# A graph attention and expert kernel: how the first two supertiles are fed, where the row sums are made, and who splits the expert weights

## The reference

```python
h = inlayer2 @ W.T + b
f1 = h @ w1 + b1
f2 = h @ w2 + b2
logits = f1[:, None] + f2[None, :]
bias_mat = NEG_BIG * (1.0 - (adj_mat > 0))
coefs = softmax(leaky_relu(logits, 0.01) + bias_mat, axis=-1)
x = x + coefs @ layernorm(x)
xf = layernorm(x)
probs = softmax(xf @ gate_w + gate_b)          # top 2 of 8 kept, as weights cw
out = x + sum_e cw[:, e] * (gelu(xf @ W1[e] + b1[e]) @ W2[e] + b2[e])
```

## Time and profile before

| | |
|---|---|
| median of 3 runs | 521.17 us (520.91 to 521.98) |
| the profiled execution: its time | 521.97 us |
| its span, first to last instruction | 520.4 us |
| busy: PE / DVE / ACT / POOL | 474.6 / 437.2 / 211.1 / 55.1 us |
| mean granted TensorE clock | 0.969 |
| DMA queues, share of 16 engines over the span | GpSimd's 34.9%, SyncE's 22.0% |

### The profile page before, as it was taken

One profiled execution on the slowest core, in us unless ns is written; L12 is line 12 of the kernel. 1 busy time (PEld: TensorE's weight loads), 2 busy tenths in 40 slices (PEclk: granted clock), 3 DMA queues, 4 the chain that ended last, 5 costly groups with the idle time before them and its releaser, 6 DMA issues.

```text
span 520.4 us, 5922 instructions
## 1 busy us (share of the span) xinstructions
PE 474.6 (91%) x1760; PEld 232.5 (45%) x1760; DVE 437.2 (84%) x720; ACT 211.1 (41%) x322; POOL 55.1 (11%) x74
## 2 busy tenths in 40 slices
PE   1997879758999999999999999789999999999996
PEld 1976434413444544444444434334434444444442
DVE  0159379999999999999999998397989898988985
ACT  0127400001011110200102114579898888888884
POOL 5000410990200101010000000000000000000000
PEclk9997979789999999999999999979999999999999
DMA  6999999970393975929500000833443575534410
GB/s 132 195 168 117 213 166 147 92 72 1 26 105 33 89 72 46 105 15 104 52 0 0 0 0 9 148 95 66 116 82 101 97 124 110 116 101 101 120 60 22
DMA packets 36432, 44.47 MB, mean 85 GB/s; under 512 B 2320, under 2 KB 24768, under 8 KB 36416
## 3 DMA queue, kind: packets, MB, share of 16 engines
q0 software_dynamic: 16896, 16.78, 34.9%
q1 hardware_dynamic: 18704, 27.46, 22.0%
q10 hardware_dynamic: 816, 0.03, 0.1%
HBM read 92.38 MB, written 2.23 MB: 182 GB/s over the span
## 4 chain that ended last, share of the span: by engine, by line
PE 65%; DVE 16%; issue 7%; DMA 5%; ACT 4%; another core or an unknown queue 1%; SPq 1%; DVEq 1%; ACTq 0%
PE bank L1007 29%; DVE c L804 7%; PE bank L1045 4%; PE bank L1047 4%; PE bank L1046 4%; PE bank L1034 4%; PE bank L1035 4%; PE bank L1036 4%; DMA share<-in_L_gnn_inlayer 2%; PE bank L953 2%; PE bank L945 2%; PE bank L928 2%; DMA share<-shares 2%; ACT mask L544 2%; DVE xs L691 2%
## 5 line engine op out<-in xcount | busy, mean ns | idle before, releaser
L1007 PE MATMUL bank<-c,Y 128*128 128x512 f32 x512 | 234.9, 610 | 18.8 <-DVE c L804 18.7
L804 DVE SCALAR_TENSOR_TENSOR c<-g_row,r_col,maskT 128x512 f32<-128x512 uint8 (+1 forms) x256 | 196.1, 806 | 14.7 <-PE bank L1007 10.7
L1007 PEld LDWEIGHTS bank<-c,Y 128*128 128x128 f32 x512 | 94.5, 193 | 140.9 <-issue 81.5
L847 DVE TENSOR_TENSOR mask<-mask,share 128x1024 f32<-128x1024 f32 x64 | 78.3, 1223 | 23.1 <-ACT mask L544 16.1
L544 ACT ACTIVATE mask<-bank,b1T 128x512 f32<-128x512 f32 x128 | 83.8, 688 | 24.0 <-PE bank L1036 22.4
L853 DVE TENSOR_TENSOR maskT<-mask,maskT 128x1024 f16<-128x1024 f32 x64 | 78.3, 1224 | 0.0
L551 ACT ACTIVATE maskT<-mask 128x1024 f16<-128x1024 f32 x64 | 67.4, 1053 | 4.1 <-DVE mask L847 4.0
L1045 PE MATMUL bank<-maskT,w2h 128*128 128x512 f16 x128 | 49.1, 383 | 6.6 <-DVE maskT L853 6.1
L1035 PE MATMUL bank<-share,w1h 128*128 (+1 forms) x128 | 49.0, 383 | 0.0
L1046 PE MATMUL bank<-maskT,w2h 128*128 128x512 f16 x128 | 49.0, 383 | 0.0
L1047 PE MATMUL bank<-maskT,w2l 128*128 128x512 f16 x128 | 49.0, 383 | 0.0
(11 more groups left out here) (143 smaller groups left out, 343.9 us busy)
## 6 DMA issues: line engine op xcount, KB each, us to landing
mask<-in_adj POOLq DMA_DIRECT2D x32, 512.0 KB, 17.7
share<-shares SPq DMA_DIRECT2D x16, 1024.0 KB, 8.2
share<-in_L_gnn_inlayer SPq DMA_DIRECT2D x8, 256.0 KB, 8.7
share<-in_x SPq DMA_DIRECT2D x8, 256.0 KB, 20.1
out<-c SPq DMA_DIRECT2D x8, 256.0 KB, 3.8
share<-in_L_ffn_W SPq DMA_DIRECT2D x1, 1024.0 KB, 22.0
x<-in_x SPq DMA_DIRECT2D x1, 256.0 KB, 10.1
W_sb<-in_L_gnn_W SPq DMA_DIRECT2D x1, 64.0 KB, 1.9
```

The lines of the kernel that those rows point to most:

```text
L804: dve.scalar_tensor_tensor(c[:, k % CR].rearrange("p (s i) -> p s i", i=32), g_row[:, bass.ds(s * ST, ST)].rearrange("p (s i) -> p s i", i ...
L847: dve.tensor_tensor(hw[:, e % 2], h[:, e % 2], wb[:, e].unsqueeze(1).to_broadcast([P, FC, ST]), ALU.mult).then_inc(hw_done, 1)
L1007: mm(bank[:, par, :], Y[:, k], c[:, k % CR], start=(k == 0), stop=(k == NK - 1)).then_inc(c_used, 1)
```

## The change

- SyncE loads inlayer2 in plain rows (partition p has rows 32p to 32p+31, 8 KB in one run of each half) with two DMAs instead of eight. ScalarE alone copies the turned blocks, and puts the columns in the mask's order on the way. TensorE makes the f columns only after all eight blocks, 32 in a row.
- The first mask is loaded in 16 pieces (four quarters of four DMAs), each quarter with a semaphore of its own; VectorE turns the quarters between steps of the start. The second mask's DMAs are issued once x has landed.
- One f1 row is made before supertile 0, the other seven behind its chunks 1, 3, ... 13. ScalarE makes their `g_row` parts after its 24 rows of Y, and then the normalized rows `xin` of x (32 instructions), over `in2_j`.
- The row sums are eight products of ones by four `xin` chunks each, behind chunks 24 to 31 of supertile 0. VectorE makes `all_h` and `all_l` itself behind chunk 2 of supertile 1 (`mean_rows`).
- x2 is one DMA. The weights are loaded after supertile 0. ScalarE makes their high parts in supertile 1, VectorE the low parts in supertile 2 behind chunks 0, 3, ... 21.
- Supertiles 1 and 2 are taken out of the loops; gate and b2 are still split on GpSimd.

```diff
@@ sync
-            for b in (0, half):
-                for q in range(Q):
-                    sp.dma_start(dst_k(in2_j, q)[:, b:b + half],
-                                 by_chunk(in2)[q].rearrange("a b e d -> a b (e d)")[:, b:b + half]).then_inc(in2_in[b // half], 16)
+            for n in range(2):
+                part = slice(n * half, (n + 1) * half)
+                sp.dma_start(in2_j[:, part], by_k(in2)[:, part]).then_inc(in2_in[n], 16)
...
             sp.wait_ge(f1row_ready, NB)
-            sp.dma_start(x2[:, 0:TS], x_rows[:, 0:TS]).then_inc(xn_in[0], 16)
-            sp.dma_start(x2[:, TS:NK], x_rows[:, TS:NK]).then_inc(xn_in[1], 16)
+            sp.dma_start(x2[:], x.rearrange("(n p) d -> p n d", p=P)).then_inc(xn_in, 16)
+            sp.wait_ge(c_used, NK)
             sp.wait_ge(y_rows, NK + 1)
             sp.wait_ge(S_ready, 1)
@@ gpsimd
-            load_adj(0, 0)
+            for p in range(NP):
+                for q in range(Q):
+                    pool.dma_start(mask[32 * q:32 * q + 32, p],
+                                   adj_v[0, q][:, PS_ * p:PS_ * p + PS_]).then_inc(adj0_in[p], 16)
+            for n in range(2):
+                pool.wait_ge(xj_in[n], 64)
             load_adj(1, 1)
...
-            pool.wait_ge(S_step, 1)
-            pool.tensor_scalar(all_rows[:], all_rows[:], ident[:, D - 1:D], None, ALU.mult).then_inc(S_step, 1)
-            pool.wait_ge(S_step, 2)
-            pool.tensor_copy(all_h[:], all_rows[:]).then_inc(S_step, 1)
-            pool.wait_ge(S_step, 3)
-            pool.tensor_tensor(all_l[:], all_rows[:], all_h[:], ALU.subtract).then_inc(all_ready, 1)
...
             load_adj(3, 1)
-            split(w1raw, w1h[:], w1l[:], arrived=(w_in, 32))
-            split(w2raw, w2h[:], w2l[:])
@@ scalar
-            for b in range(1, NB, 2):
+            in2T_t = in2T.rearrange("d (b e q a1 a0) -> d a0 e q b a1", a0=8, e=4, q=Q, b=NB)
+            for b in range(NB):
                 act.wait_ge(in2t_ready, b + 1)
...
+                    if p == 6 and isinstance(s, int) and s == 1:
+                        act.wait_ge(w_in, 32)
+                        for raw, hi in ((w1raw, w1h[:]), (w2raw, w2h[:])):
+                            act.activation(hi, raw, ACT.Copy, scale=W_SCALE).then_inc(whi_made, 1)
...
             supertile(0, 0, first=True)
-            with act.Fori(0, NS // 2 - 1) as i:
+            for b in range(1, NB):
+                g_part(b)
+            for k in range(NK):
+                act.activation(xin[:, k], x_j[:, k], ACT.Identity, bias=nmrs[:, k:k + 1],
+                               scale=rs1[:, k:k + 1]).then_inc(xin_made, 1)
@@ vector
-            for b in range(0, NB, 2):
-                dve.wait_ge(in2t_ready, b + 1)
-                dve.tensor_copy(in2T[:, ST * b:ST * b + ST], bank[:, TURN[b % 4], :]).then_inc(in2t_dve, 1)
...
+                    if isinstance(s, int) and s == 1 and k == 2:
+                        mean_rows()
...
+                    if isinstance(s, int) and s == 2 and k % 3 == 0 and k < 24:
...
+                        dve.wait_ge(whi_made, v + 1)
+                        ins = dve.scalar_tensor_tensor(lo, raw, W_SCALE, hi, ALU.mult, ALU.subtract)
...
+            def mean_rows():
+
+                dve.wait_ge(S_ready, 1)
+                dve.wait_ge(pool_const, 1)
+                link(dve.tensor_reduce(all_rows[:], bank[:, 3, :].rearrange("p (e d) -> p d e", d=D), AX_X, ALU.add))
+                link(dve.tensor_scalar(all_rows[:], all_rows[:], ident[:, D - 1:D], None, ALU.mult))
+                link(dve.tensor_copy(all_h[:, 0:D], all_rows[:]))
+                dve.tensor_tensor(all_l[:, 0:D], all_rows[:], all_h[:, 0:D], ALU.subtract).then_inc(all_ready, 1)
@@ tensor
-            for k in range(NK):
-                ins = mm(bank[:, 3, P:P + D], rs1[:, k:k + 1].to_broadcast([P, P]), x_j[:, k],
-                         start=(k == 0), stop=(k == NK - 1))
-            ins.then_inc(S_ready, 1)
+            def row_sum(n):
+                pe.wait_ge(xin_made, 4 * n + 4)
+                return mm(bank[:, 3, :], ones[:], xin[:, 4 * n:4 * n + 4].rearrange("p k d -> p (k d)"),
+                          start=(n == 0), stop=(n == NK // 4 - 1))
...
+                    if first and k >= NK - NK // 4:
...
+                        ins = row_sum(k - NK + NK // 4)
...
+                    if first and k % 2 == 1 and k // 2 + 1 < NB:
+                        f1_row(k // 2 + 1)
```

More of the change, by code:

```diff
@@ L170, in gnn_moe_kernel @@
         out_sb = c[:, 1, :].rearrange("p (t d) -> p t d", d=D)
+        xin = in2_j
         in2T = x2[:, :, :].rearrange("p k d -> p (k d)")
@@ L181, in gnn_moe_kernel @@
         xj_in = [sem(f"xj_in{i}") for i in range(2)]
-        xn_in = [sem(f"xn_in{i}") for i in range(2)]
+        xn_in = sem("xn_in")
         w_in = sem("w_in")
         adj_in = [sem(f"adj_in{i}") for i in range(2)]
+        adj0_in = [sem(f"adj0_in{i}") for i in range(4)]
         pool_const = sem("pool_const")
@@ L207, in gnn_moe_kernel @@
         S_ready = sem("S_ready")
+        xin_made = sem("xin_made")
         all_ready = sem("all_ready")
@@ L211, in gnn_moe_kernel @@
         wsplit = sem("wsplit")
+        gate_split = sem("gate_split")
+        whi_made = sem("whi_made")
         b1_ready = sem("b1_ready")
@@ L285, in _ @@
         def _(sp):
-            half = NB // 2
+            half = NK // 2
             sp.dma_start(W_sb[:], gnn_w).then_inc(small_in, 16)
@@ L391, in _, with split @@
             splits = [0]
-            def split(raw, hi, lo, arrived=None):
-                if arrived is not None:
-                    pool.wait_ge(*arrived)
+            def split(raw, hi, lo, done):
                 n, splits[0] = splits[0], splits[0] + 1
@@ L614, in turn @@
             def turn(n, p, par):
-                dve.wait_ge(adj_in[par], 64 * n)
+                if isinstance(n, int) and n == 0:
+                    dve.wait_ge(adj0_in[p], 64)
+                else:
+                    dve.wait_ge(adj_in[par], 64 * n)
                 dve.transpose(at32v[:, par, PS_ * p:PS_ * p + PS_, :].rearrange("p s w -> p (s w)"),
@@ L623, in stats @@
                 return ins
-            dve.wait_ge(xj_in[0], 64)
-            stats(0, B1)
+            for n in range(2):
+                dve.wait_ge(xj_in[n], 64)
+                last = stats(n * B1, (n + 1) * B1)
+                if n == 0:
+                    turn(0, 0, 0)
+            link(last)
+            for k in range(NK):
+                ins = dve.bn_aggr(mv1[:, k], st1[:, k])
+            ins.then_inc(mv1_ready, 1)
+            turn(0, 1, 0)
             dve.wait_ge(fcol_made, 1)
-            f12 = bank[:, 4, 2 * P:2 * P + 2 * NK].rearrange("p (k v) -> p v k", v=2)
+            f12 = bank[:, 4, 32:32 + 2 * NK].rearrange("p (k v) -> p v k", v=2)
             dve.tensor_copy(f1_col[:], f12[:, 0])
@@ L671, in _ @@
                 row_chunk(k)
-            for p in range(2, NP):
-                turn(1, p, 0)
+            turn(0, 3, 0)
             POST = 3
@@ L797, in supertile @@
                         dve.wait_ge(turned, (s + 1) * NP)
-                    if first and k == 0:
-                        dve.wait_ge(grow_ready, NB)
+                    if k == 0:
+                        dve.wait_ge(grow_ready, 1 if first else NB)
                     need(dve, c_used, s * NK + k - CR + 1)
@@ L834, in supertile @@
                         next(router, None)
+            def mean_rows():
[5 more added lines that the diff above has]
+                dve.tensor_tensor(all_l[:, 0:D], all_rows[:], all_h[:, 0:D], ALU.subtract).then_inc(all_ready, 1)
             supertile(0, 0, 1, first=True)
-            with dve.Fori(0, NS // 2 - 1) as i:
-                supertile(i * 2 + 1, 1, i + 2)
+            supertile(1, 1, 1)
+            supertile(2, 0, 2)
+            with dve.Fori(1, NS // 2 - 1) as i:
+                supertile(i * 2 + 1, 1, i + 1)
                 supertile(i * 2 + 2, 0, i + 2)
```

130 lines of the change are left out of this document (63 added, 67 removed).

## The result

| | before | changed |
|---|---|---|
| median (lowest to highest), 4 runs each | 521.29 us (520.91 to 521.98) | 513.25 us (512.68 to 513.80) |
| span of the profiled execution | 520.4 us | 511.5 us |
| mean granted clock | 0.969 | 0.965 |

The ratio is 0.9844, with a 95% interval of 0.9827 to 0.9861: 8.0 us faster.

The account below looks back on a forecast made before the run. TensorE, then VectorE, nearly fill ordinary supertiles; GpSimd's splits and the wait for mask 1 cost extra. The -8.9 at supertile 3 and +0.5 gave -8.4: 513.6 from 521.97, 512.8 from the median; said 513.0, range 508.5 to 518.

Parts of the forecast that it names:

- Mask 1: Supertile 0: with x2, weights and mask 2 packets held back, mask 1 lands at 58.7 us, chunk 8 comes 7.1 earlier.
- the 1.1 us: Loads ahead of mask 1: 112 packets of mask 2 no longer moved before it, 1.1 us.
- rival 2: First mask in pieces is slower: 12 added DMAs make mask 1 8 us later, time 521; chance 0.05.
- End of supertile 0: TensorE done at 93.7 us: 91.2, less 7.1 for mask 1, plus 9.6 for three f1 rows and eight row sums.
- Rival 1: The start decides, not mask 1: supertile 0 ends at 95.2 or 98 us, time 514.5 to 517; chance 0.16.
- The start: Before supertile 0: first chunk at 51.6 us, supertile 0's end at 95.2, nearly level with mask 1's 93.7.
- Row sums into supertile 1: mean_rows takes 1.6 us, the rest of supertile 1 28.3; supertile 2 begins at 123.6 instead of 136.99, -13.4 in sum.
- Splits: High parts 4.2 us, hidden in supertile 1; low parts add 5.4 in supertile 2; supertile 3 at 159.4, -8.9.
- rival 4: More gain than forecast: low parts fall half into TensorE's time and mean_rows is cheap, 510 us; chance 0.11.
- After that: From supertile 3 on: TensorE bounds again with a shorter queue, +0.5 us given back; experts untouched.

Follow-up runs that it names:

- e9: The kernel before, with one wait added so that x2 and the weights load only after the first quarter of mask 1 is turned: 513.12 us.
- e10: The kernel before, with x2 and the weights held behind mask 1's first turn and the weight splits moved to ScalarE and VectorE: 501.71 us.
- e1: The changed kernel with the weight splits back on GpSimd and ScalarE's high and VectorE's low parts taken out: 524.25 us.
- e6: The changed kernel with the first mask in four DMAs instead of 16, all quarters waiting for the whole mask: 520.73 us.
- e3: The changed kernel without GpSimd's wait for x before it issues mask 1: 510.11 us.
- e2: The changed kernel with f1 rows reading in2T in runs of 32 adjacent columns and ScalarE ordering them as it writes g_row: 506.93 us.
- e5: The changed kernel with inlayer2 in eight DMAs of 2 KB a partition instead of two of 8 KB: 517.22 us.
- e4: The changed kernel with f1 rows read in runs of 32 columns and no wait for x before mask 1 is issued: 509.13 us.

## Why the prediction was right

It said 513.0 us, range 508.5 to 518; measured 513.25. The two causes hold by experiment (e9 and e10 for mask 1, e1 and e10 for the splits). That the number met the measured one within 0.3 us is luck: at supertile 3 the gain was 1.9 us short of the forecast, because the end of supertile 0 came later than said, and an unforecast gain of 1.9 us in the experts made up for it (in the profiled pair).

- **Mask 1, -7.1 predicted.** Chunk 8 came 8.1 us earlier, and mask 1 was in at 58.56 for the 58.7 of the sum. The cause is shown by e9, 6.4 us from the bytes in front of it; the sizes of the parts were off and cancelled. Mask 2 was issued at 50.06 us, earlier than before (60.86), so its packets were not out of the way: 133 of them had been moved by 58.5 us (4549 packets, less 2 x 2112 and the 192 that the pieces add), and the 1.1 us did not come. The faster start made up for it: by 56 us GpSimd's queue had moved 4.07 MB here and 3.92 in e9, beside the same 4.26 MB of SyncE's. The twelve more DMAs that rival 2 charged with 8 us cost nothing that shows (e6: 4.18 MB by 57 us with and without them).
- **End of supertile 0, "93.7 us"** (95.79 measured). This is the step that was wrong in kind: it let the mask decide, and took every wide product at 0.87 us. Four terms: chunk 8 ready 1.0 us sooner than I said; no gap, so none of the 1.6 to 1.9 us of slow clock (e9, e10) that stood unseen in the 91.2 us from the earlier trace rows; three f1 rows at 1.73 instead of 0.87, +2.6; TensorE, late from the start and from four earlier f1 rows, at chunk 8 only at 62.88 instead of 60.6, +2.3. That makes 2.0 to 2.3 for 2.1 measured. Rival 1's mechanism was therefore the true one, with a start earlier than its 51.6 us (first chunk at 46.3) and longer rows; the 512 columns alone did not fix an f1 row's price.
- **The start**, priced for a first chunk at 51.6 us, had it at 46.31: x came 7.4 us sooner, and GpSimd's late reduction (2.97 us of VectorE's time, e3) was not foreseen. Even so TensorE, and not the mask, decided.
- **Row sums into supertile 1.** `mean_rows` took 1.5 us (predicted 1.6), and the rest of the supertile 28.5 (28.3). No chunk there took over 0.75 us.
- **Splits.** High parts 1.9 us each (2.1), hidden. Supertile 2 was to take 35.8 us (30.4 of VectorE's work and waits, and 5.4 of low parts) and took 35.4. A low part has a record of 0.69 us, but the next instruction begins 0.60 us after it, so the eight are 4.8:

```profile
126.51 0.69 DVE L849 SCALAR_TENSOR_TENSOR w1l<-share,w1h 128x512 f16<-128x512 f32 x1
127.11 2.07 DVE L822 SCALAR_TENSOR_TENSOR c<-g_row,r_col,maskT 128x512 f32<-128x512 f32 x3
```

  Over an ordinary supertile of 31.3 they cost 4.1, since part of them falls into VectorE's slack, as rival 4 had it; the 30.4 of the sum had already counted 0.9 of that slack.
- **After that.** Supertile 3 began 7.0 us ahead of before instead of 8.9, and stayed so: 7.07 us at supertile 4. The "+0.5 given back" did not come.
- **A gain that was not forecast.** At VectorE's last chunk of supertile 7 the profiled pair is 7.0 us apart (325.35 and 318.32), at its first product of the experts 7.8 (334.39 and 326.57), and the spans 8.9. The difference comes in the experts' start, where before's profiled run also had a clock 0.08 lower for 21 us (0.84 and 0.92). That execution lay 0.7 us over its median, so part of it is that one run; the rest was not tried.

The prediction asked what the whole change gives, and not what each part gives alone. The two removed losses are worth some 20 us (e10), and some 11 to 12 of them are paid back by work moved from ahead of the stall to behind it: the row sums, 8 x 0.86 = 6.9 us, and the f1 rows, 3 x 1.73 = 5.2 us behind chunk 8. With the 0.4 us by which TensorE reaches chunk 8 later (62.88 and 62.47) that makes the 12.5 us between the two kernels at supertile 3. The f1 rows' part was tried (e2); that of the row sums is this sum alone, no run moved them by themselves.

## What to carry to other kernels

When an engine stands for a transfer, sum what was issued ahead of that transfer on every queue and hold back what isn't wanted yet: here one wait was worth 7.9 us by the medians, 3.6 to 8.9 by the interval. Work that sits in front of a stall is free, and costs its full time once it is moved behind it; count that before making room for anything. Take elementwise work off GpSimd where VectorE runs two-input instructions, and measure the two causes apart before rebuilding a start around them.

## What the runs showed of the hardware

- Float32 matmul records of 512 columns follow each other at half the pace when neighbouring columns of the moving operand lie 512 bytes apart: 1048 ns a record and 0.87 us apart, against 592 ns and 0.43 with runs of 32 neighbours (e2) or a plain operand (L982), at a granted clock of 1.00.
- GpSimd began its reduction over the partitions 6.71 us after issuing DMAs, and its next elementwise instruction 8.82 us after that reduction (7.46 before, 7.77 in e3), with no releaser in the trace. When the issue lay long enough ahead (21 us in e3, 14 in e6) the first delay did not appear.
- Beside a stream of 1 KB packets, a load of 2 MB in runs of 8 KB got 1.22 MB through in 4 us, the same load in runs of 2 KB 0.79 MB, and x behind it landed 3.4 us sooner (e5).
- A mask of 2 MB in 16 DMAs of 128 KB, queued one behind the other, was moved as fast as in 4 of 512 KB (e6: 4.18 MB of two masks by 57 us either way).
- Behind gaps of TensorE of 1.40 (e2), 2.76 (e9) and 3.11 us (e10) its granted clock stayed at 1.00; behind gaps of 3.78 (e4) and 5.99 us (before) the table has stretches of 6 us at 0.72 and 0.50. These are single executions; the gaps differ also in what ran ahead of them.
